# Rows of maxima copied by two engines, and products of the identity between two layers

## What is computed

```
qkv = norm(x) @ w_qkv.T              # 12 query heads, 4 key and value heads, repeated 3 times
logits = q . k / sqrt(32)            # over the 49 keys of each query's window
a = softmax(logits)
x = x + (a . v) @ w_out.T
```

## Time and profile before

| | us |
|---|---|
| median of 3 runs | 1131.62 (1129.42 to 1133.83) |
| profiled execution | 1136.01 |
| its span, first to last instruction | 1134.4 |
| PE busy | 1008.4 (89%) |
| DVE busy | 510.9 (45%) |
| POOL busy | 389.7 (34%) |
| ACT busy | 330.3 (29%) |
| TensorE's mean granted clock | 0.954 of full speed |

### The profile page before, as it was taken

One profiled execution on the slowest core, in us unless ns is written; L12 is line 12 of the kernel. 1 busy time (PEld: TensorE's weight loads), 2 busy tenths in 40 slices (PEclk: granted clock), 3 DMA queues, 4 the chain that ended last, 5 costly groups with the idle time before them and its releaser, 6 DMA issues.

```text
span 1134.4 us, 13376 instructions
## 1 busy us (share of the span) xinstructions
PE 1008.4 (89%) x4377; PEld 583.3 (51%) x4378; DVE 510.9 (45%) x898; ACT 330.3 (29%) x494; POOL 389.7 (34%) x333
## 2 busy tenths in 40 slices
PE   6999999999981599999297888899998999999998
PEld 3755545555440366665155555477444555555554
DVE  4565687788562145554643564671111111111114
ACT  2514545554611121221325455151111111111100
POOL 5514667677735101000523657353000000000014
PEclk9999999999996799999598899999998999999999
DMA  8689408000067236411434200603444424411015
GB/s 294 149 262 287 93 3 184 1 1 1 1 227 284 77 140 230 145 56 41 118 95 112 57 1 1 246 33 111 146 153 153 153 93 178 174 48 35 14 35 153
DMA packets 47177, 130.07 MB, mean 115 GB/s; under 512 B 7121, under 2 KB 26073, under 8 KB 46872
## 3 DMA queue, kind: packets, MB, share of 16 engines
q1 hardware_dynamic: 32360, 65.05, 19.6%
q0 software_dynamic: 14768, 64.37, 16.2%
HBM read 87.78 MB, written 30.61 MB: 104 GB/s over the span
## 4 chain that ended last, share of the span: by engine, by line
PE 74%; DVE 7%; issue 7%; DMA 5%; ACT 4%; POOL 1%; SPq 0%; POOLq 0%; DVEq 0%; ACTq 0%
PE PS L1759 22%; PE PS L1780 10%; PE PS L1561 6%; PE PS L1610 5%; PE PS L1487 5%; PE PS L1732 4%; DMA Wd<-in_Wd_r 4%; PE PS L1591 4%; DVE nmax_part L1236 3%; PE PS L1593 3%; PE PS L1696 3%; PE PS L1806 3%; ACT QB L1021 2%; DVE exp_acc L1268 2%; PE PS L1541 2%
## 5 line engine op out<-in xcount | busy, mean ns | idle before, releaser
L1759 PE MATMUL PS<-Wgu,xbT 128*128 x690 | 288.3, 560 | 10.4 <-DMA Wd<-in_Wd_r 6.6
L1759 PEld LDWEIGHTS PS<-Wgu,xbT 128*128 128x128 f32 x690 | 128.8, 193 | 130.7 <-issue 118.1
L1043 ACT ACTIVATE expS<-PS 128x1024 f32<-128x1024 f32 (+3 forms) x156 | 135.9, 878 | 120.0 <-PE PS L1593 119.0
L1780 PE MATMUL PS<-Wd,hidT 128*128 x414 | 143.1, 491 | 1.5 <-DVE hidT L1387 0.8
L842 POOL TENSOR_TENSOR exp_acc<-exp_acc,expS 128x512 f32<-128x512 f32 (+1 forms) x65 | 124.4, 1914 | 47.6 <-ACT expS L1043 46.7
L1591 PE MATMUL PS<-QA,KS 128*128 128x512 f32 (+3 forms) x312 | 119.1, 386 | 17.6 <-ACT QB L1021 17.6
L1236 DVE TENSOR_REDUCE nmax_part<-PS 128x1 f32<-128x512 f32 x160 | 103.7, 685 | 46.0 <-PE PS L1561 45.1
L1561 PE MATMUL PS<-KS,QA 128*128 128x512 f32 (+2 forms) x288 | 110.2, 429 | 10.6 <-DVE nmax L1236 2.6
L1593 PE MATMUL PS<-QB,KS 128*128 128x512 f32 (+3 forms) x312 | 114.7, 372 | 0.0
L1780 PEld LDWEIGHTS PS<-Wd,hidT 128*128 128x128 f32 x414 | 79.0, 192 | 57.6 <-issue 14.4
L946 POOL DMA_INDIRECT got<-block_rows_out,row_i x32 | 31.2, 976 | 207.6 <-DMA block_rows_out<-yb 198.4
(11 more groups left out here) (171 smaller groups left out, 1224.8 us busy)
## 6 DMA issues: line engine op xcount, KB each, us to landing
Wgu<-in_Wgu POOLq DMA_DIRECT2D x8, 1152.0 KB
Wgu<-in_Wg_r POOLq DMA_DIRECT2D x8, 1152.0 KB
Wgu<-in_Wu_r POOLq DMA_DIRECT2D x8, 1152.0 KB
Wd<-in_Wd_r POOLq DMA_DIRECT2D x8, 1152.0 KB
xb<-block_rows_in SPq DMA_DIRECT2D x46, 192.0 KB, 2.4
block_rows_out<-yb SPq DMA_DIRECT2D x46, 192.0 KB, 1.8
part_rows<-parts SPq DMA_DIRECT2D x2, 3072.0 KB, 17.6
Wd<-in_Wd POOLq DMA_DIRECT2D x8, 576.0 KB
```

The source lines that it names most:

```text
L1043: act.activation(exp_tile(layer, c, unit)[:, pair, :].rearrange("p (b n) -> p b n", b=2)[:, :, lo:hi], PS[:, 2 * pair:2 * pair + 2, lo:hi] ...
L1759: last = pe.matmul(PS[:, 3 * par + lo // BANK, 0:n], xbT[:, par, kc, :], Wgu[layer][:, bass.ds(s, 1), kc, lo:lo + n], start=kc == 0, stop= ...
L1780: last = pe.matmul(PS[:, 7, 0:C], hidT[layer][:, par, i, :], Wd[layer][:, bass.ds(s, 1), i, :], start=i == 0, stop=i == m.IC - 1)
```

## The change

In layer 1 the rows of heads 2 and 3 are copied by VectorE instead of ScalarE, with a semaphore of their own (`nmax_dve`); the copies stand in VectorE's list behind the last maxima and before the reciprocals. TensorE makes the rows of maxima before the weighted values of unit 3 instead of behind them, and piece 14 is done in unit 2 instead of unit 3. Between the layers TensorE multiplies the identity with itself, 6 products into bank 5 whenever a tile's two gathers have come (for the first four tiles) and 2 when the variance of these tiles is there. Layer 0's attention stays as it is.

```diff
-        PIECES_TO = [0, 5, 10, 14, 16, 16]
+        PIECES_TO = [0, 5, 10, 15, 16, 16]
...
 (ScalarE, copy_rows)
+                    if layer and pair:
+                        return
                     rows = 1 if layer == 0 else D
...
 (VectorE)
+                def copy_rows(hb):
+                    c = hb // HALF % KC
+                    dve.wait_ge(nmax_psum, hb + 1)
+                    if hb == BLOCKS:
+                        dve.wait_ge(b_early, 16 * G)
+                    else:
+                        dve.wait_ge(b_in[c % 2], placed(B_DMAS, 1, c))
+                    for g in range(2, G):
+                        last = dve.tensor_copy(QB[1][c % 2][D:2 * D, g, hb % HALF * BANK:(hb % HALF + 1) * BANK],
+                                               PS[D * g:D * g + D, 4, :])
+                    last.then_inc(nmax_dve, 1)
...
                 maxima(first_block, range(TILES))
+                if layer:
+                    copy_rows(first_block)
...
+                            if layer and v == ROWS_AT[1]:
+                                copy_rows(hb + 1)
                         if v == ROWS_AT[layer] and hb > first_block:
                             reciprocals(hb - 1, 1)
...
 (TensorE)
+            def keep_busy(bank, count):
+                for n in range(count):
+                    pe.matmul(PS[:, bank, 0:P], ident[:, :], ident[:, :], start=True, stop=True)
...
             for layer in range(2):
+                if layer:
+                    for t in range(4):
+                        pe.wait_ge(got_in[t], 32)
+                        keep_busy(5, 6)
+                    pe.wait_ge(var_ready, 5)
+                    keep_busy(5, 2)
                 transposes(2 * layer)
...
 (max_piece, first piece of a block)
-                            pe.wait_ge(nmax_act, 2 * hb)
+                            pe.wait_ge(nmax_act, 2 * hb if layer == 0 else hb + BLOCKS)
+                            if layer:
+                                pe.wait_ge(nmax_dve, hb - BLOCKS)
...
 (scores, first unit of a block)
-                        pe.wait_ge(nmax_act, 2 * (BLOCKS * layer + HALF * c + half) + pair + 1)
+                        if layer == 0:
+                            pe.wait_ge(nmax_act, 2 * (HALF * c + half) + pair + 1)
+                        elif pair == 0:
+                            pe.wait_ge(nmax_act, 2 * BLOCKS + HALF * c + half + 1)
+                        else:
+                            pe.wait_ge(nmax_dve, HALF * c + half + 1)
...
 (the loop over units)
+                        if layer and v == ROWS_AT[1] and not last_block:
+                            maxima_rows(coming)
                         weighted(c, u)
                         if layer and some[2:3]:
                             max_piece(coming, some[2])
-                        if layer and v == ROWS_AT[1] and not last_block:
-                            maxima_rows(coming)
```

More of the change, by code:

```diff
@@ L308, in build @@
         nmax_act = sem("nmax_act")
+        nmax_dve = sem("nmax_dve")
         score_psum = sem("score_psum")
```

## The result

Six runs of the changed kernel gave a median of 1121.93 us (1120.59 to 1123.47), six of the kernel before beside them 1130.52 (1128.76 to 1136.11): a ratio of 0.9926, 95% interval 0.9900 to 0.9952. By the ratio it is 8.4 us faster, by the medians 8.6; the forecast was 1121.6. The profiled execution took 1120.67 us, its span is 1119.1, TensorE's mean granted clock 0.966.

What follows compares the result with a forecast made beforehand. Attention bound by TensorE's waits for ScalarE's copies of the maxima rows, plus lost clock and waits between the layers. 6.7 + 2.5 + 0.75, some 10.0 us, off 1136.0 gives 1126.0, forecast as a 1121.6 median; range 1114.5 to 1128.5.

Steps and rivals of the forecast that it cites:

- my signs of being wrong: Layer 1's attention: second to fourth blocks less than 3 us under 59.2, or VectorE's maxima starting with TensorE waiting for them.
- the attention's waits: Attention of layer 1: shorter waits for copies gain 0.5 + 4 x 1.38 + 0.7 = 6.7 us.
- its clock: Attention of layer 1: less idling makes the second block like the fourth, gaining 2.5 us, bounds 0 and 6.
- the products: Between the layers: products of the identity raise TensorE's clock, gaining 0.75 us, bounds 0 and 3.4.
- my 0.7: Last attention block: half the boundary's gain, between 0 and 1.38, as POOL starts later while TensorE comes 1.4 earlier.
- The rival by which the clock holds everywhere: Attention and between the layers: less idling everywhere, terms 6.7 + 6 + 3.4 = 16.1, 1115.5 us; chance 0.24.
- the 1.4 us of my sum: Between the layers: at the full clock the projection's first 2.8 us shrink by 1.4.
- The other 2 us of my upper bound: Between the layers: another 2 us if ScalarE's third copy was waiting for slow transposes.
- The order of the rows: Block boundaries: rows ahead of the weighted values win only cover; priced at 0, 0 to 0.3 either way per boundary.
- The wait did pass on in part: Rival, attention: the wait passes to VectorE and POOL, 5.2 of 6.7 us go, about 1129 us; chance 0.17.
- The copies do run side by side on one bank: Rival, attention: copies on both engines don't run side by side, only cover is left, about 1130 us; chance 0.06.
- The clock did not fall at the boundaries between blocks: Rival, attention: the clock falls at every boundary and stays down, 8.1 us slower, 1139.7 us; chance 0.05.

Runs made afterwards that it cites:

- experiment 2: Kernel before with only the products of the identity added between the layers; 1133.77 us, ratio 1.0013.
- experiment 4: Kernel before with only TensorE's order changed (rows ahead of the weighted values, piece 14 in unit 2), all copies on ScalarE, no products; 1129.49 us, ratio 0.9976.
- Experiment 8: Kernel before with VectorE's copies alone, plus POOL's normalisation of the tenth block moved behind the last block's second addition; 1120.35 us, ratio 0.9883.
- before: The kernel without the change; median 1130.52 us, profiled execution 1136.0 us.
- (3): Kernel before with only the copies of heads 2 and 3 on VectorE, old order and pieces, no products; 1118.94 us, ratio 0.9885.
- (11): Changed kernel with the first 24 products all behind the fourth tile's gathers, two behind the variance; 1124.21 us, one run.
- experiment 9: Changed kernel with TensorE's five waits between the layers but none of the 26 products; 1126.54 us, one run.
- (5): Changed kernel with one tiny ScalarE activation, waiting for nothing, between the square root and the copies of the transposes; 1122.35 us once.
- (10): Changed kernel with one product at each of the five places, 5 in place of 26; 1122.66 us, one run.
- (6): Changed kernel with 9 products of 384 columns in place of 26 of 128; 1124.69 us once.
- after: The changed kernel with all parts of the change; median 1121.93 us, ratio 0.9926, profiled execution 1120.67 us.
- (7): Changed kernel with all 26 products ahead of the gathers, without a wait; 1119.17 us once.
- (1): Changed kernel without the products of the identity; 1124.65 us, ratio 0.9935.

## Why the prediction was right, and where it was not

**Right in its mechanism.** Each engine makes two copies, side by side, and the second pair's wait is gone. The rows still start 0.05 us behind the last maximum. The reciprocal comes 2.7 us later against t0 (t0 - 1.21 in the earlier trace rows, 635.68 = t0 + 1.49 now; 2.6 forecast). The second to fourth blocks take 51.20 us instead of 59.2. Of my signs of being wrong, TensorE's wait for maxima at the start of a block shows only in the fourth, with 0.76 us where it was 0.31; in the third it is 0.49 where it was 0.53.

**Lucky in its number.** The forecast was 10.0 us of gain, and 8.6 were measured; 1121.93 comes so near to 1121.6 because the kernel before had a median of 1130.52 in these runs and not 1131.62. The three terms were off by more, and both ways: the attention's waits by -1.9, its clock by +3.5, the products by -4.0.

**The attention's waits: 6.7 forecast, about 4.8 found.** A boundary gives 1.17, not 1.38; the third and the fifth block, whose clock is up in both profiles, show it alone. The missing 0.2 lies in the second pair of scores: the old unit's exponential ends at 636.06, and they start at 636.21 = t0 + 2.02, where I had t0 + 1.85. The first block gives 0.4 of its 0.5 (16.73 and 16.76 in experiments 2 and 4, where its clock is up and its copies are still ScalarE's, against 16.32). The last gives nothing: my 0.7 took it that POOL is only half late. POOL waited 1.97 us for the reciprocal behind VectorE's copies, TensorE waited 2.29 for POOL, and the clock fell. Experiment 8 confirms it: there the wait is 0.86 us shorter, and the block gains that and some clock. So 0.4 + 4 x 1.17 - 0.25 = 4.8, if the second and fourth blocks' waits shrink like the third's (the -0.25 of the last block holds its clock too). For the second block three profiles with ScalarE's copies bear this out: it took 21.50, 20.18 and 18.85 us with 10.2, 6.8 and 3.4 us at half clock, so about 17.5 with none, by this line (an estimate); 16.37 is 1.2 less.

**The clock: 2.5 forecast, about 6.0 found,** the upper bound. It is what is left: 10.8 - 4.8; 1.5 in the first block, 4.0 in the second, 0.5 in the fourth. It is no accident of one profile: in all ten profiles with VectorE's copies the second to fifth blocks have no half clock, in the three with ScalarE's alone they have 13.7, 6.8 and 10.2 us. The rival by which the clock holds everywhere was the better account of this term. Part of the 6.0 is that the profiled execution of before, 1136.01 us, is at the upper end of that kernel's runs, with 20.5 us at half clock in the attention where experiment 2 had 10.2 with the same waits; this goes some way to explain why the medians differ by less than the profiles. The page "TensorE: Matmul & The Clock Gate" of the Trainium skill, section "A second HAM failure mode: psum-queue depth-cycling", would have had the clock go on swinging; here one wait of 0.66 to 0.87 us was left at each boundary, and the trace doesn't agree: 1.00 through five of six blocks. With one wait of 1.31 (3) it held too, with 0.66 to 0.87 and a second of 0.96 to 1.10 (4) it fell: what goes with the held clock in these runs is that the second wait is gone.

**The products: the step that failed.** I took a gain of 0.75, between 0 and 3.4, and found a loss of 3.2 in the stage. Two things were missing. I had counted their time on TensorE (right: they end ahead of the transposes) but put at nothing that they could make what follows late, so my lower bound excluded a loss without a reason. And the clock that they raise is gone again by 558, so the projection begins at half clock as before. Where it did stay up (11), the projection gained the 1.4 us of my sum. The other 2 us of my upper bound, for the third copy, were not won where that copy was in time: in experiment 9 the copies follow each other without a long wait, and the stage is only 0.3 shorter, as the projection then runs longer at half clock.

What the runs show of the loss: ScalarE is ready (5). Against before, the projection's start is put off by nothing where there are only waits (9) or 5 products (10), by 0.7 us with 9 wide products (6), by 2.9 to 4.2 with 26 small ones (after, 2, 11), and by nothing with 26 ahead of the gathers (7). So it goes with the number of instructions that TensorE goes through while the gathers run, and not with their columns. Each of these kernels was profiled once.

How it comes about stays open. In experiments 2 and 11 TensorE idles ahead of instructions that wait for nothing. But in after and in experiment 5 its transposes are on record in time, and it is the copies waiting for them that start 2.8 and 2.7 us late; in before the third copy starts 1.67 us behind the last transpose without any product. So either the records are not the whole of what TensorE does, or its signals are held up as well. That TensorE waits for its instructions to be loaded is one reading, and no view shows it: a packet of 0.02 MB on the queue named "instruction" comes between 548 and 550 in after, 556 and 558 in experiment 11, 538 and 540 in experiment 7. In after that is 8 us or more before the first copy could have come, in experiment 11 some 5 us before TensorE's first idle time: not in the stalls. It takes 1.3 and 1.1 us there, no longer than the 1.4 in experiment 7, where no gather runs beside it. The Trainium skill's page "Runtime: NRT & Kernel Launch", section "Instruction fetch mechanics", has the engine fetch its next block of instructions by DMA while it runs the current one, mostly hidden. The packet agrees with the fetching; whether the stall is a fetch that was not hidden, no run here shows. In time the products alone cost 1.5 us (-0.1 to 2.9), less than the stage, and leaving them out of the changed kernel saved nothing (1). So the loss is shown for the stage; what gives some of it back in time stays open.

**The order of the rows** was priced at 0, and in the attention it is: what one wait loses another gains (4), and without the order the attention is the same (3). In time it is not settled. Experiments 1 and 3 differ in the order (with piece 14) alone, and their ratios, 0.9911 to 0.9960 with it and 0.9865 to 0.9906 without, don't overlap, while by experiment 4 the order is a gain. Where the 5.7 us between their medians lie stays open: the two changed stages are the same to 0.1 us in their profiles, and the unchanged end took 420.4 and 417.1 us, with 4.2 and 0.7 us at half clock.

**The rivals.** The wait did pass on in part, to POOL, and the last block lost by it. That TensorE's waits for maxima doubled to 5.2 us comes mostly from the order of the rows: with the copies alone they are 3.1 us (3), with the order alone 4.7 (4). The copies do run side by side on one bank. The clock did not fall at the boundaries between blocks.

## What to carry to other kernels

When one engine copies for two waiting consumers, look for an engine with slack behind the same release and give it half, and then follow what it delays to the last user, here POOL's sums at the end of the stage. If an engine has two short waits in a row, the one to remove may be worth more than its length, as the clock was here. Products that keep TensorE busy are not free just because TensorE has time: here 26 of them cost nothing only ahead of the transfers, and gained nothing there. Check the first real instructions behind them. Where the clock swings between executions, compare single stages whose clock is up in both, since the spans of two profiles can be further apart than the kernels (15.3 against 8.6 us here).

## What the runs showed of the hardware

ScalarE and VectorE copied different partitions of one PSUM bank at the same time: two copies of 32x512 took 1.19 us on ScalarE, as alone, and 1.40 on VectorE, 0.70 each, above my bounds of 0.54 to 0.65. What VectorE's would take alone no run shows.

The clock held from the second to the fifth block with one wait a boundary, of 0.66 to 0.87 us or of 1.31 (3), where with two waits it fell in some blocks: 20.5 us of the attention were at half clock in before and 10.2 in experiment 2, with waits of 1.30 to 1.31 and 0.96 to 1.10, and 17.1 in experiment 4, with 0.66 to 0.87 and 0.96 to 1.10. A wait of 2.29 us at the attention's end was followed by a fall at once in after and not in experiment 6.

Behind 24 or more small products during the gathers TensorE's next instructions came 0.7 to 1.4 us apart in two runs (559.69, 560.42, 561.86 and 562.57 in experiment 2; 563.25, 564.65 and 565.41 in experiment 11, while the DMA share fell from 0.51 to 0.29). In two others the instructions came in time, and the copies that wait for them started 2.7 to 2.8 us behind the last one's end.
